# The epsilon of four variances moved from ScalarE to GpSimd, with a new order of all steps, in a four-layer attention kernel

## The chip, the cores and the metric

One core of one Trainium2 chip runs the whole program. The metric is the time of one execution on the device, in microseconds (us); lower is better. Engines are called by the names of the profile: PE is TensorE (matmuls and transposes through a matmul with the identity), PEld its loading of weights, DVE is VectorE, ACT is ScalarE, POOL is GpSimd, SP is SyncE, whose instruction queue SPq issues every DMA of this kernel. The PE clock that the throttle granted was full (2.4 GHz) in the whole stage that matters, so nothing below is about the clock.

## What is computed

Four layers of cross-attention over 64 batch elements of 128 tokens with 256 features. The keys and values of all four come from `ctx_512` (128 features); the second layer also attends to a side input. Cut to what matters (`softmax` over keys in L0, L1 and L3, over tokens in L2):

```python
def attn(q, k, v): return softmax(q @ k.T * scale) @ v
def ln(x, g, b, eps): return (x - mean(x)) * rsqrt(var(x) + eps) * g + b

# L0
x = x + attn(x@Wq+bq, ctx@Wk+bk, ctx@Wv+bv) @ Wo + bo
# L1: two attentions, on ctx and on the side input; eps = 1e-5
x1n = ln(x, ln1_g, ln1_b)
out = x + sum(attn(x1n@Wq+bq, ln(s)@Wk+bk, ln(s)@Wv+bv) @ Wo + bo for s in (ctx, side))
x = ln(out, ln_g, ln_b) @ fc_W + fc_b + out
# L2: eps = 1e-6
x = ln(x + attn_over_tokens(x, ctx), gamma, beta)
# L3
x = x + attn(x@Wq+bq, ctx@Wk+bk, ctx@Wv+bv) @ Wo + bo
```

So there are four kinds of variance, which the kernel calls `keys` (of ctx and side), `ln1` (of the queries of L1), `lnf` (in front of fc) and `ln2` (the end of L2). Each needs `(var + eps) ** -0.5`.

## The kernel before

The 64 batch elements are worked on in 32 groups of two (`GROUPS`, `GROUP`; numbers g from 0 to 31). For each group about 100 named steps run, each on one engine: for example `Q_L0` (queries of L0) on PE, `exp_L1` on ACT, `out_L0` on DVE, `lo_L0` on POOL. The steps of up to a dozen groups are under way together. Ahead of and among the first groups stand the preparations (`PREPARATIONS`): weights are loaded, multiplied with each other (`M_L0`, `N_L1a`, ...), centred and split into a high and a low part.

The order is written out by hand in tables: `STARTS` has a number for each step and group, `PREPARATIONS` one for each preparation. `timetable()` sorts all of them, and each engine gets its own steps in that sequence. The numbers do nothing but sort; no instruction waits for a time. `SEATS` says which of the 8 PSUM banks a PE step fills. `COPIES` says how many buffers a tile has, and a step waits (`earlier`) until the buffer that it takes is free. Between engines every step waits for the semaphores of those it reads (`done[...]`).

The reciprocal roots are made as follows. For `keys`, `lnf` and `ln2`, DVE takes `bn_stats` and `bn_aggr` (`moments`, L1407; the second raises `mean_k`), ACT adds epsilon (`eps_of`, L1118, one `ACTIVATE` with the tile `epsilon` as its bias, which writes `var_eps`), POOL raises it to the power -0.5 (`rstd_of`, L1646, the instruction at L1655). For `ln1` the sum comes from `out_L0`; DVE turns it into `less_mean_ln1` (L1447), ACT squares and sums (`eps_ln1`, L1135), then scales by 1/256 and adds epsilon in a further `ACTIVATE` (L1140), and POOL takes the power. What follows is `shift_keys` (L1464) and `shift_ln2` (L1472) on DVE, `norm_side` (L1664) and `norm_ln2` (L1674) on POOL, `norm_ctx` (L1230) and `norm_ln1` (L1238) on ACT, and `out_fc` (L1507) on DVE. An epsilon step has 128x2 or 128x4 values.

All DMAs are issued by SP in the order of the table: the loads of weights and of the first groups, then, among the loads, each group's trips through HBM that turn a tile (`send_keys` and `fetch_keys`, `send_x3` and `fetch_x3`, `send_xhat` and `fetch_xhat`), and `store`. At the start the table has SP load ctx of group 0, the weights of L2's queries and keys (`load_qk_L2`), two rows, and the columns of small vectors (`load_cols`, one DMA with 34 values a partition). PE begins with `run_up` (L802), then `M_L2` (L784), `k_L2` (L794, which needs DVE's `scaled` of the columns), `B2` of group 0 (L865, which needs both parts of `M_L2`, made by ACT and DVE), `M_L0` (L706).

Of the kernel before, what the change touches and what calls it, by code (L numbers as in the profile page):

```python
# [1793 lines left out]
```

## Time and profile before

| | us |
|---|---|
| median of 3 runs | 564.6 (562.73 to 564.97) |
| the profiled execution | 563.27 |
| its span, from first to last instruction | 561.4 |

| engine | busy us | share | instructions |
|---|---|---|---|
| PE | 545.0 | 97% | 4308 |
| PEld | 524.9 | 93% | 4308 |
| DVE | 479.8 | 85% | 1533 |
| ACT | 479.7 | 85% | 1698 |
| POOL | 416.0 | 74% | 545 |

A matmul with float32 operands is recorded as two, so the counts of PE are above those of the program. A PE record overlaps the next one, since the array is pipelined: the ends are modelled, and a busy PE is one that always had something under way. The 16 DMA engines carry 92.3 MB at 164 GB/s on average.

### The profile page before, as it was taken

The page shows a single profiled execution, that of the slowest core. Times are in us where ns is not written, and L with a number is a line of the kernel's source. Part 1 is how long each engine was busy: PE and PEld are TensorE (multiplying, and loading weights), DVE is VectorE, ACT ScalarE, POOL GpSimd, SP SyncE. Part 2 cuts the span into 40 slices and gives each one's busy share as a digit, 9 for nine tenths or more (in the row PEclk, how much of TensorE's full clock was granted, in tenths as well). Part 3 has the DMA queues.
Part 4 walks back from the last instruction along what each step waited for, and adds up shares of the span by engine and source line. Part 5 has one row for each costly group of instructions (what it writes and reads, how often), then busy time and mean ns, then how long its engine had stood idle before and what let it go on. Part 6 is the DMA issues. An engine that isn't in the chain of part 4 may idle for free.

```text
span 561.4 us, 16080 instructions
## 1 busy us (share of the span) xinstructions
PE 545.0 (97%) x4308; PEld 524.9 (93%) x4308; DVE 479.8 (85%) x1533; ACT 479.7 (85%) x1698; POOL 416.0 (74%) x545
## 2 busy tenths in 40 slices
PE   7998999999999999999999999999999999999985
PEld 6998999999999999999999999999999999999974
DVE  1697689998999989988898998999997979889963
ACT  3798998899988999989989799979879998897643
POOL 3799567888858969587896878866998657365781
PEclk9999999999999999999999999999999999999999
DMA  8994254555475455654547553655476334333332
GB/s 237 361 298 157 85 162 139 174 172 158 148 219 187 145 171 169 207 165 160 165 151 238 158 165 113 215 191 167 146 211 187 110 123 133 109 99 115 95 95 75
DMA packets 100648, 92.30 MB, mean 164 GB/s; under 512 B 10576, under 2 KB 76496, under 8 KB 100560
## 3 DMA queue, kind: packets, MB, share of 16 engines
q1 hardware_dynamic: 100560, 91.29, 51.5%
q8 instruction: 36, 0.59, 0.4%
q14 instruction: 52, 0.43, 0.3%
HBM read 58.74 MB, written 32.51 MB: 163 GB/s over the span
## 4 chain that ended last, share of the span: by engine, by line
PE 83%; POOL 3%; issue 3%; DMA 3%; DVE 3%; ACT 3%; SPq 1%; DVEq 0%; POOLq 0%; ACTq 0%
PE bank L828 10%; PE bank L841 9%; PE bank L835 9%; PE bank L852 5%; PE bank L854 5%; PE bank L853 5%; PE bank L962 5%; PE bank L1005 5%; PE bank L819 5%; PE bank L811 4%; PE bank L984 4%; PE bank L865 3%; PE bank L937 3%; PE bank L938 3%; PE bank L939 3%
## 5 line engine op out<-in xcount | busy, mean ns | idle before, releaser
L1114 ACT ACTIVATE prob_L<-bank,neg_max_L 128x128 f32<-128x128 f32 x320 | 114.6, 376 | 13.3 <-DVE neg_max_L L1480 12.9
L1655 POOL TENSOR_TENSOR rstd_ln<-var_eps_ln,minus_half 128x2 f32<-128x2 f32 x64 | 45.2, 706 | 35.8 <-ACT var_eps_ln L1124 17.8
L1114 ACT ACTIVATION_READ_ACCUMULATOR prob_L<-bank,neg_max_L 128x1 f32 x320 | 69.0, 216 | 0.0
L1480 DVE TENSOR_REDUCE neg_max_L<-bank 128x2 f32<-128x256 f32 (+1 forms) x128 | 60.4, 476 | 6.4 <-PE bank L835 4.8
L1040 ACT ACTIVATE oT_hi_L<-bank 128x256 fp32r<-128x256 f32 (+1 forms) x96 | 44.0, 461 | 12.8 <-PE bank L841 11.1
L1293 DVE TENSOR_TENSOR oT_lo_L<-bank,oT_hi_L 128x256 fp32r<-128x256 f32 (+1 forms) x96 | 47.8, 499 | 7.3 <-ACT oT_hi_L L1040 6.6
L1040 ACT ACTIVATE probT_L<-bank 128x256 f32<-128x256 f32 (+1 forms) x96 | 43.3, 460 | 12.2 <-PE bank L819 11.9
L1703 POOL TENSOR_TENSOR x_bias<-x,bias_fc 128x512 f32<-128x512 f32 x32 | 41.0, 1281 | 15.3 <-DVE x L1513 15.1
L1696 POOL TENSOR_TENSOR x_in<-x_in,bias_L 128x512 f32<-128x512 f32 x32 | 41.1, 1287 | 11.0 <-DMA x_in<-in_x 11.0
L1513 DVE TENSOR_TENSOR x<-bank,x 128x512 f32<-128x512 f32 x64 | 43.3, 679 | 6.5 <-issue 3.3
L1688 POOL TENSOR_TENSOR xT_lo_L<-xT_in,xT_hi_L 128x512 fp32r<-128x512 f32 x32 | 41.2, 1288 | 7.2 <-ACT xT_hi_L L1040 7.1
L819 PE MATMUL bank<-ident,prob_L 128*128 128x128 f32 x256 | 43.0, 274 | 0.3 <-ACT prob_L L1114 0.2
L1718 POOL TENSOR_TENSOR x_res<-xhat_ln,gamma_row 128x512 f32<-128x512 f32 x32 | 41.1, 1286 | 2.7 <-DVE y L1507 2.1
L1720 POOL TENSOR_TENSOR x_res<-x_res,bias_L 128x512 f32<-128x512 f32 x32 | 41.1, 1284 | 2.5
L852 PE MATMUL bank<-N_hi_L,oT_hi_L 128*128 128x256 f32 x128 | 40.7, 318 | 2.1 <-DVE oT_lo_L L1293 2.1
L1245 ACT ACTIVATE prob_L<-prob_L,inv_total_L 128x128 f32<-128x128 f32 x128 | 41.1, 409 | 0.7 <-DVE inv_total_L L1487 0.5
L1655 POOL TENSOR_TENSOR rstd_keys<-var_eps_keys,minus_half 128x4 f32<-128x4 f32 x32 | 32.6, 1018 | 10.6 <-ACT var_eps_keys L1124 5.2
L835 PE MATMUL bank<-ctx_in,qT_L 128*128 128x128 f32 x256 | 39.3, 276 | 0.3
L841 PE MATMUL bank<-probT_L,ctx_in 128*128 128x128 f32 x256 | 39.0, 277 | 0.6 <-ACT probT_L L1040 0.5
L1674 POOL TENSOR_SCALAR xhat_ln<-x,rstd_ln,shift_ln 128x256 f32<-128x256 f32 x64 | 35.1, 555 | 5.1 <-DVE shift_ln L1472 3.0
L937 PE MATMUL bank<-F_hi,xT_hi_fc 128*128 128x256 f32 x128 | 38.0, 297 | 0.1
L1507 DVE SCALAR_TENSOR_TENSOR y<-bank,inv_total_L,x_res 128x256 f32<-128x256 f32 x64 | 27.8, 476 | 9.6 <-PE bank L854 8.0
(238 smaller groups left out, 2251.0 us busy)
## 6 DMA issues: line engine op xcount, KB each, us to landing
ctx_in<-in_ctx SPq DMA_DIRECT2D x32, 256.0 KB, 3.3
xT_in<-in_x SPq DMA_DIRECT2D x32, 256.0 KB, 3.3
x_in<-in_x SPq DMA_DIRECT2D x32, 256.0 KB, 3.1
keys_out<-keys_turned SPq DMA_DIRECT2D x32, 256.0 KB, 2.3
keysT<-keys_out SPq DMA_DIRECT2D x128, 64.0 KB, 2.1
out<-y SPq DMA_DIRECT2D x32, 256.0 KB, 2.2
x_out<-x_turned SPq DMA_DIRECT2D x30, 256.0 KB, 2.2
x3T<-x_out SPq DMA_DIRECT2D x120, 64.0 KB, 2.1
```

Source lines behind the costliest of these rows:

```text
L819: last = tr(block(bank, b), src[:, b, :], ident[:])
L828: last = mm(bank[:, i * TOK:(i + 1) * TOK], w[:, t, :], x[:, t, :], start=t == 0 and n == 0, stop=t == T - 1 and n == 2)
L835: last = mm(block(bank, b), block(at(qT[k], g), b), kT[:, b], start=True, stop=True)
L841: last = mm(block(bank, b), natural[:, b, :], block(at(probT[k], g), b), start=True, stop=True)
L852: mm(to, h, N_h[:], start=i == 0, stop=False)
L937: mm(to, hi[:, t, s], F_hi[:, t, :], start=t == 0, stop=False)
L1040: activation(to, of, ACT.Copy).then_inc(done[step], 1)
L1114: last = activation(at(prob[k], g)[:, b, :], block(bank, b), ACT.Exp, bias=at(neg_max[k], g)[:, b:b + 1], accum_out=at(total[k], g)[:, b:b ...
L1293: dve.tensor_tensor(to, of, hi.bitcast(F32), ALU.subtract).then_inc(done[step], 1)
L1480: dve.tensor_reduce(at(neg_max[k], g)[:], scores, AX.X, ALU.max, negate=True).then_inc(done[f"max_{k}"], 1)
L1513: dve.tensor_tensor(flat(at(to, g)), bank_of(use, g)[:], flat(at(add, g)), ALU.add).then_inc(done[step], 1)
L1655: pool.tensor_tensor(at(rstd[k], g)[:], at(var_eps[k], g)[:], minus_half[:, 0:n], ALU.pow).then_inc(done[f"rstd_{k}"], 1)
```

## The change

The epsilon steps leave ACT. `eps_of` and the last instruction of `eps_ln1` are gone, with the two tiles `epsilon` and their memsets; what is left of `eps_ln1` is a step of its own name, `squares_ln1`. In `rstd_of`, POOL now waits for `mean_k` (or `squares_ln1`), adds epsilon with a `tensor_scalar` from one SBUF tile (two operations, multiply and add, for `ln1`), waits for its own write, and takes the power. DVE's `bn_aggr` waits for the buffer's last reader, now `rstd_k` instead of `eps_k`.

All tables (`STARTS`, `PREPARATIONS`, `SEATS`) have new numbers; `COPIES` has not. The new sequence differs most in the first transfers and the preparations. Behind that, the places of most steps change by a few, and the last steps on PE stand in the old sequence.

```diff
-            def eps_of(k, eps):
-                def of(g):
-                    if g == 0:
-                        prepared(act, "constants")
-                    act.wait_ge(done[f"mean_{k}"], g + 1)
-                    earlier(act, f"rstd_{k}", g, len(var_eps[k]))
-                    activation(at(var_eps[k], g)[:], at(mean_var[k], g)[:, :, 1], ACT.Identity,
-                               bias=epsilon[eps][:, 0:1]).then_inc(done[f"eps_{k}"], 1)
-                return of
...
-                act.wait_ge(done["squares_ln1"], g + 1)
-                earlier(act, "rstd_ln1", g, len(var_eps["ln1"]))
-                activation(at(var_eps["ln1"], g)[:], at(squares_ln1, g)[:], ACT.Identity, bias=epsilon[EPS_L1][:, 0:1],
-                           scale=1.0 / D).then_inc(done["eps_ln1"], 1)
...
-                earlier(dve, f"eps_{k}", g, len(mean_var[k]))
+                earlier(dve, f"rstd_{k}", g, len(mean_var[k]))
...
-            def rstd_of(k, used_by):
-                def of(g):
+            def rstd_of(k, used_by, epsilon, of):
+
+                def rstd_k(g):
                     if g == 0:
                         prepared(pool, "constants")
+                    pool.wait_ge(done[of], g + 1)
+                    if k == "ln1":
+                        pool.tensor_scalar(at(var_eps[k], g)[:], at(squares_ln1, g)[:], 1.0 / D, epsilon, ALU.mult, ALU.add).then_inc(done[f"eps_{k}"], 1)
+                    else:
+                        pool.tensor_scalar(at(var_eps[k], g)[:], at(mean_var[k], g)[:, :, 1], epsilon, None, ALU.add).then_inc(done[f"eps_{k}"], 1)
                     pool.wait_ge(done[f"eps_{k}"], g + 1)
...
-    "load_qk_L2": 118, "load_cols": 310, "load_rows_wkv_L1v": 214, "load_qk_L1v": 406, "load_qk_L0": 502, "load_v_L2": 598,
...
+    "load_qk_L2": 70, "load_rows_wkv_L1v": 598, "load_cols": 214, "load_qk_L1v": 502, "load_qk_L0": 310, "load_v_L2": 406,
```

How the order moves. First, SP at the start of the program, before and then after (line numbers of the changed kernel are lower by 7 to 21; `WqT_L2` is the weight of L2's queries, `WqT_L0` that of L0's):

```order
L640 DMA ctx_in_0<-in_ctx 128x512
L577 DMA WqT_L2<-in_L2_WqT 128x2x256
L577 DMA WkT_L2<-in_L2_WkT 128x2x128
L581 DMA row_L1v_g2<-in_rows 128x128
L581 DMA row_L1v_b2<-in_rows 128x128
L600 DMA cols<-in_cols 128x34
L644 DMA side_in_0<-in_side 128x256
```

```order
L570 DMA WqT_L2<-in_L2_WqT 128x2x256
L570 DMA WkT_L2<-in_L2_WkT 128x2x128
L633 DMA ctx_in_0<-in_ctx 128x512
L593 DMA cols<-in_cols 128x34
L627 DMA xT_in_0<-in_x 128x512
L570 DMA WqT_L0<-in_L0_WqT 128x2x256
L570 DMA WkT_L0<-in_L0_WkT 128x2x128
```

The weights of L2 now go first instead of second and third, and the columns fourth instead of sixth; the two rows and the side input are later.

Second, PE at the start of the program, behind `run_up`: before and then after (`WqT_L,WkT_L` is `M_L2`, `ctxT_hi,M2T_hi` and the like are `B2` of group 0, `scaled_cols,WqT_L` is `k_L2`):

```order
L784 MATMUL bank<-WqT_L,WkT_L 128x256 x2
L794 MATMUL bank<-scaled_cols,WqT_L 128x1 x4
L865 MATMUL bank<-ctxT_hi,M2T_hi 128x256
L865 MATMUL bank<-ctxT_hi,M2T_lo 128x256
L865 MATMUL bank<-ctxT_lo,M2T_hi 128x256
```

```order
L777 MATMUL bank<-WqT_L,WkT_L 128x256 x2
L858 MATMUL bank<-ctxT_hi,M2T_hi 128x256
L858 MATMUL bank<-ctxT_hi,M2T_lo 128x256
L858 MATMUL bank<-ctxT_lo,M2T_hi 128x256
L858 MATMUL bank<-ctxT_hi,M2T_hi 128x256
L858 MATMUL bank<-ctxT_hi,M2T_lo 128x256
L858 MATMUL bank<-ctxT_lo,M2T_hi 128x256
L787 MATMUL bank<-scaled_cols,WqT_L 128x1 x4
L699 MATMUL bank<-WkT_L,WqT_L 128x128 x4
```

`B2` of group 0 now stands ahead of `k_L2`; `M_L0` (`WkT_L,WqT_L`) follows both as before.

Third, POOL some 40 instructions in, where the first groups of L0 and L1 overlap the preparations: before and then after (`rstd_ln1_1` is the buffer 1 of `rstd_ln1`):

```order
L1688 TENSOR_TENSOR xT_lo_L0_0<-xT_in_1,xT_hi_L0_0 128x512
L1664 TENSOR_SCALAR keys_2<-side_in_2,rstd_keys_0 128x128 x2
L1682 TENSOR_TENSOR ctxT_lo_0<-ctx_in_4,ctxT_hi_0 128x256
L1655 TENSOR_TENSOR rstd_ln1_1<-var_eps_ln1_1,minus_half 128x2
L1655 TENSOR_TENSOR rstd_keys_1<-var_eps_keys_1,minus_half 128x4
L1655 TENSOR_TENSOR rstd_ln1_0<-var_eps_ln1_0,minus_half 128x2
```

```order
L1661 TENSOR_TENSOR ctxT_lo_0<-ctx_in_4,ctxT_hi_0 128x256
L1643 TENSOR_SCALAR keys_2<-side_in_2,rstd_keys_0 128x128 x2
L1628 TENSOR_SCALAR var_eps_ln1_1<-squares_ln1_1 128x2
L1634 TENSOR_TENSOR rstd_ln1_1<-var_eps_ln1_1,minus_half 128x2
L1619 TENSOR_TENSOR row_L3_bo<-row_L3_bo,row_L3_b1 128x256
L1630 TENSOR_SCALAR var_eps_keys_1<-mean_var_keys_1 128x4
L1634 TENSOR_TENSOR rstd_keys_1<-var_eps_keys_1,minus_half 128x4
L1628 TENSOR_SCALAR var_eps_ln1_0<-squares_ln1_0 128x2
L1634 TENSOR_TENSOR rstd_ln1_0<-var_eps_ln1_0,minus_half 128x2
```

Each power now has its epsilon in front of it on the same engine, 128 of them in the program, and a row of the preparations (`row_L3_bo`) has moved in among them.

## Rows read from the trace of the kernel before

**Rows 1.** The page, busy time of each engine, share of the span, instructions.
```profile
PE 545.0 (97%) x4308; PEld 524.9 (93%) x4308; DVE 479.8 (85%) x1533; ACT 479.7 (85%) x1698; POOL 416.0 (74%) x545
```

**Rows 2.** Stretches: length, busy us (instructions) of PE, PEld, DVE, ACT, POOL; clock, DMA, GB/s.
```profile
0.00:20.00 20.00, 16.67 (x77) 15.13 (x78) 5.96 (x23) 7.99 (x19) 9.52 (x27) 1.00 0.89 272
20.00:50.00 30.00, 29.42 (x219) 27.73 (x220) 24.41 (x93) 28.13 (x94) 27.65 (x36) 1.00 0.89 285
50.00:80.00 30.00, 27.95 (x231) 26.84 (x230) 22.91 (x77) 27.86 (x97) 19.17 (x23) 1.00 0.37 117
...
100.00:520.00 420.00, 418.39 (x3404) 407.66 (x3403) 380.54 (x1200) 379.30 (x1361) 319.63 (x412) 1.00 0.52 162
520.00:561.00 41.00, 33.16 (x231) 29.19 (x230) 27.07 (x82) 19.34 (x68) 24.60 (x32) 0.98 0.28 89
```

**Rows 3.** Groups of ACT: the epsilon steps; busy us, mean ns, idle before <-releaser.
```profile
L1124 ACT ACTIVATE var_eps_keys<-mean_var_keys,epsilon 128x4 f32<-128x4 f32 x32 | 9.9, 311 | 2.1 <-DVE mean_var_keys L1416 2.1
L1124 ACT ACTIVATE var_eps_lnf<-mean_var_lnf,epsilon 128x2 f32<-128x2 f32 x32 | 9.8, 307 | 1.9 <-DVE mean_var_lnf L1416 1.8
L1124 ACT ACTIVATE var_eps_ln<-mean_var_ln,epsilon 128x2 f32<-128x2 f32 x32 | 9.7, 303 | 0.9 <-DVE mean_var_ln L1416 0.7
L1140 ACT ACTIVATE var_eps_ln<-squares_ln,epsilon 128x2 f32<-128x2 f32 x32 | 9.5, 296 | 1.0
```

**Rows 4.** The same view of POOL.
```profile
L1655 POOL TENSOR_TENSOR rstd_ln<-var_eps_ln,minus_half 128x2 f32<-128x2 f32 x64 | 45.2, 706 | 35.8 <-ACT var_eps_ln L1124 17.8 <-ACT var_eps_ln L1140 17.7
...
L1720 POOL TENSOR_TENSOR x_res<-x_res,bias_L 128x512 f32<-128x512 f32 x32 | 41.1, 1284 | 2.5
...
L1674 POOL TENSOR_SCALAR xhat_ln<-x,rstd_ln,shift_ln 128x256 f32<-128x256 f32 x64 | 35.1, 555 | 5.1 <-DVE shift_ln L1472 3.0 <-issue 2.1
...
L1664 POOL TENSOR_SCALAR keys<-side_in,rstd_keys 128x128 f32<-128x128 f32 x64 | 23.2, 375 | 9.1 <-PE bank L841 8.8 <-POOL rstd_keys L1655 0.4
...
L1588 POOL MEMSET one<- 128x1 f32 x1 | 0.1, 99 | 0.0
```

**Rows 5.** The power (L1655) on POOL by stretch: length, busy (instructions), clock, DMA, GB/s.
```profile
20.00:50.00 30.00, 6.08 (x7) 1.00 0.89 285
...
100.00:520.00 420.00, 79.73 (x103) 1.00 0.52 162
```

**Rows 6.** Timeline at the start: start us, us, what [idle before <-releaser]; SP, ACT, PE.
```profile
1.66 0.46 SPq L577 DMA_DIRECT2D WkT_L<-in_L_WkT  x1
...
7.81 0.39 ACT L1104 ACTIVATE M2T_hi<-bank 128x256 fp32r<-128x256 f32 x1 [3.95 <-PE bank L784]
...
5.70 2.08 PE L784 MATMUL bank<-WqT_L,WkT_L 128*128 128x256 f32 x4 [1.79 <-DMA WkT_L<-in_L_WkT]
8.34 1.87 PE L794 MATMUL bank<-scaled_cols,WqT_L 128*128 128x1 f32 x8 [0.56 <-DVE scaled_cols L1297]
```

**Rows 7.** The chain that ended last: start us, us, what.
```profile
3.14 4.93 DMA cols<-in_cols
...
38.32 0.30 ACT var_eps_ln L1140
...
39.43 1.03 POOL M_lo_L1a L1627
...
48.55 1.03 POOL rstd_keys L1655
```

**Rows 8.** Timelines of DVE, POOL and PE from 49 to 53 us.
```profile
49.62 2.46 DVE L1464 SCALAR_TENSOR_TENSOR shift_keys<-mean_var_keys,rstd_keys,one 128x1 f32<-128x1 f32 x2
...
49.53 1.30 POOL L1688 TENSOR_TENSOR xT_lo_L<-xT_in,xT_hi_L 128x512 fp32r<-128x512 f32 x1
50.77 1.28 POOL L1696 TENSOR_TENSOR x_in<-x_in,bias_L 128x512 f32<-128x512 f32 x1
...
52.73 0.39 PE L828 MATMUL bank<-xT_hi_L,M_hi_L1a 128*128 128x256 f32 x1 [1.46 <-DVE xT_lo_L L1293]
```

**Rows 9.** Line L1464 of DVE: duration ns min/median/max.
```profile
L1464 DVE SCALAR_TENSOR_TENSOR shift_keys<-mean_var_keys,rstd_keys,one x64: 176/213/1306, 11.3 to 475.8; 128x1 f32<-128x1 f32 x64
```

More of the change, by code:

```diff
@@ new lines @@
+    "rstd_keys": [1426, 2077, 2870, 4535, 5226, 5809, 6545, 7370, 8941, 11613, 13273, 14563, 15378, 16048, 18933, 20861, 21391,
[59 rows of a table added]
+    "T_fc": [5972, 6945, 7838, 9006, 10690, 13100, 14169, 15159, 16461, 18051, 20719, 21677, 23079, 24381, 26606, 27727, 29880,
[3 rows of a table added]
+    "hi_fc": [6185, 7069, 7905, 9069, 10798, 13178, 14234, 15292, 16553, 18178, 20790, 21823, 23187, 24444, 26718, 27819, 29973,
+        30998, 33455, 35009, 35786, 36720, 38447, 40383, 42823, 44998, 45831, 46724, 48787, 49725, 50647, 51348],
@@ new lines @@
+    "OUT_fc": [6433, 7219, 8042, 9341, 11099, 13748, 14531, 15618, 16778, 18423, 21086, 22206, 23555, 24831, 27302, 28242,
+        30238, 31568, 33917, 35260, 35966, 37221, 38884, 40633, 43090, 45232, 46107, 46886, 49034, 49877, 51056, 51751],
+    "out_fc": [6600, 7381, 8284, 9523, 11262, 13923, 14719, 15780, 17053, 18629, 21496, 22369, 23717, 25078, 27482, 28481,
[33 rows of a table added]
+    "x_res": [8678, 10145, 11350, 12602, 13873, 16857, 18598, 19245, 20472, 21527, 24086, 25678, 27197, 27997, 30482, 32080,
[17 rows of a table added]
+    "store": [10772, 12223, 14749, 15490, 19065, 20202, 20763, 22614, 23234, 26797, 27151, 29011, 29428, 32031, 34357, 35378,
[7 rows of a table added]
@@ L234 @@
-PREPARATIONS = {"run_up": 154, "M_L2": 461, "k_L2": 669, "M_L0": 950, "m_L0": 1039, "M_L1v": 1104, "n_fc": 1193, "mean_fc": 1280,
[14 rows of a table removed]
[1 row of a table added]
+    "turn_xhat": [8617, 10047, 11115, 12500, 13830, 16761, 17934, 19263, 20036, 21342, 24115, 25608, 27133, 28296, 30402, 32118,
+        33773, 34676, 38056, 38891, 39860, 41329, 41806, 43709, 45632, 47893, 49087, 50432, 51582, 52152, None, None],
+    "send_xhat": [8694, 10181, 11313, 12606, 13908, 16839, 18012, 19392, 20250, 21420, 24414, 25758, 27210, 28435, 30479, 32196,
+        33851, 34754, 38133, 38969, 39970, 41465, 41932, 43787, 46053, 47970, 49165, 50510, 51660, 52230, None, None],
@@ new lines @@
+    "fetch_xhat": [9032, 10447, 11578, 12927, 14173, 17104, 18285, 19658, 20571, 21758, 24824, 26024, 27499, 28771, 30877,
[5 rows of a table added]
+    "shift_keys": [1570, 2245, 3014, 4719, 5381, 6026, 6942, 7930, 9126, 11757, 13518, 14797, 15669, 16247, 19089, 21462, 22082,
+        22905, 25374, 26721, 28559, 29540, 30602, 33189, 34601, 36857, 38175, 38275, 40990, 42704, 44183, 45478],
+    "norm_ctx": [1615, 2290, 3125, 5601, 6448, 7164, 8575, 10358, 12984, 13734, 14528, 15952, 17992, 20285, 20964, 22664, 24010,
+        26044, 27069, 29179, 30214, 32640, 34329, 35313, 35919, 37839, 39566, 42140, 43887, 45094, 45879, 48015],
@@ new lines @@
+    "norm_side": [1574, 2603, 4286, 5614, 6289, 7193, 8429, 10640, 12971, 14136, 14700, 15873, 17584, 20028, 21103, 22621,
+        23898, 26047, 27927, 29130, 30170, 32603, 34286, 35395, 35922, 37955, 39472, 42187, 43957, 45049, 45852, 48218],
+    "load_xT": [262, 1366, 1414, 1462, 2374, 3046, 3620, 4103, 4917, 5628, 7806, 9464, 10639, 12010, 12558, 14845, 15810, 17344,
[3 rows of a table added]
+}
+PREPARATIONS = {"run_up": 154, "M_L2": 421, "k_L2": 868, "M_L0": 1045, "m_L0": 1364, "M_L1v": 1628, "n_fc": 1453, "mean_fc": 1540,
[14 rows of a table added]
@@ L251 @@
 SEATS = {
     "M_L2": [0],
-    "k_L2": [1],
-    "B2": [2, 3, 6, 1, 6, 2, 4, 3, 4, 5, 1, 3, 0, 6, 7, 3, 6, 4, 2, 1, 6, 1, 2, 2, 6, 6, 0, 7, 0, 1, 5, 6],
+    "k_L2": [2],
+    "B2": [1, 6, 7, 3, 3, 4, 0, 0, 0, 7, 2, 1, 7, 7, 0, 3, 3, 5, 7, 6, 4, 3, 1, 0, 7, 6, 2, 4, 3, 2, 0, 6],
     "M_L0": [3],
-    "m_L0": [4],
-    "M_L1v": [5],
+    "m_L0": [5],
+    "M_L1v": [0],
     "n_fc": [6],
     "mean_fc": [7],
[26 rows of a table removed]
-    "T_fc": [5, 0, 2, 6, 1, 3, 5, 0, 6, 7, 5, 6, 4, 0, 1, 7, 2, 7, 1, 0, 3, 3, 2, 0, 6, 6, 3, 1, 4, 0, 2, 1],
@@ L346 @@
 ONLY_LATE = ("hi_L2", "xT_L3")
-SMALL = [f"{what}_{k}" for what in ("stats", "mean") for k in ("keys", "lnf", "ln2")] + ["squares_ln1"] + ["x_gamma", "zeroed", "small"]
+SMALL = [f"{what}_{k}" for what in ("stats", "mean") for k in ("keys", "lnf", "ln2")] + [f"eps_{k}" for k in ("keys", "ln1", "lnf", "ln2")] + ["x_gamma", "zeroed", "small"]
 def timetable():
@@ L386, in build @@
         scaled_cols = sb("scaled_cols", [P, len(COLS), T])
-        epsilon = {e: sb(f"epsilon_{i}", [P, 1]) for i, e in enumerate((EPS_L1, EPS_L2))}
         gamma_row = sb("gamma_row", [P, D])
@@ L1116, in exponentials, with squares_ln1_of @@
                 last.then_inc(done[f"exp_{k}"], 1)
[L1118 to L1131 removed]
+            def squares_ln1_of(g):
                 act.wait_ge(done["less_mean_ln1"], g + 1)
                 earlier(act, "T_L1", g, len(xhat["ln1"]))
+                earlier(act, "rstd_ln1", g, len(squares_ln1))
                 for b in range(GROUP):
@@ L1281, in scalar_program @@
                       "hi_L1": hi_of("L1", "Q_L1"), "hi_fc": hi_of("fc", "OUT_fc"),
-                      "xT_L3": xT_L3, "eps_keys": eps_of("keys", EPS_L1), "eps_ln1": eps_ln1,
-                      "eps_lnf": eps_of("lnf", EPS_L1), "eps_ln2": eps_of("ln2", EPS_L2)},
+                      "xT_L3": xT_L3, "squares_ln1": squares_ln1_of},
                      {f"M_hi_{a}": M_hi_of(a) for a in ATTENTIONS if a != "L3"} | {f"N_hi_{a}": N_hi_of(a) for a in ATTENTIONS}
@@ L1445, in mean_ln1 @@
                 dve.wait_ge(done["out_L0"], g + 1)
-                earlier(dve, "eps_ln1", g, len(less_mean_ln1))
+                earlier(dve, "squares_ln1", g, len(less_mean_ln1))
                 dve.tensor_scalar(at(less_mean_ln1, g)[:], at(sum_ln1, g)[:], -1.0 / D, None, ALU.mult).then_inc(done["less_mean_ln1"], 1)
@@ L1585, in constants @@
                                    channel_multiplier=1)
-                for eps, tile in epsilon.items():
-                    pool.memset(tile[:], eps)
                 pool.memset(one[:], 1.0)
@@ L1720, in x_res_of @@
                 pool.tensor_tensor(at(x_res, g)[:], at(x_res, g)[:], every(bias["L3"]), ALU.add).then_inc(done["x_res"], 1)
-            steps_of({"rstd_keys": rstd_of("keys", "norm_side"), "rstd_ln1": rstd_of("ln1", "norm_ln1"),
-                      "rstd_lnf": rstd_of("lnf", "out_fc"), "rstd_ln2": rstd_of("ln2", "norm_ln2"),
+            steps_of({"rstd_keys": rstd_of("keys", ["norm_side", "norm_ctx"], EPS_L1, "mean_keys"), "rstd_ln1": rstd_of("ln1", ["norm_ln1"], EPS_L1, "squares_ln1"),
+                      "rstd_lnf": rstd_of("lnf", ["out_fc"], EPS_L1, "mean_lnf"), "rstd_ln2": rstd_of("ln2", ["norm_ln2"], EPS_L2, "mean_ln2"),
                       "norm_side": norm_side, "norm_ln2": norm_ln2, "lo_ctx": lo_ctx, "lo_L0": lo_L0,
```

82 lines of the change are left out of this document (27 added, 55 removed), and 401 rows, old and new, of tables (PREPARATIONS, SEATS, STARTS).

## The prediction

> **What bounds the kernel now.** I read the page first. PE is busy for 545.0 of 561.4 us and no other engine above 85% [rows 1]. A share is an average, so next come the stretches [rows 2]. From 100 to 520 us PE is busy for 418.39 of 420 us: there it sets the pace, and all that the other engines do differently can bring 1.6 us there at most. The rest of PE's idle time lies at the two ends. In the first 20 us it is 20 - 16.67 = 3.3 us, from 20 to 50 us 0.6, from 50 to 80 us 2.05, and behind 520 us 7.8 us. So the ends are what a new order can win or lose.
>
> In these ends other engines are near their limit. From 20 to 50 us ACT is busy for 28.13 us and POOL for 27.65 us of 30; from 50 to 80 us ACT still for 27.86, POOL for only 19.17 [rows 2]. The chain that ended last says which of them counts: from 39.43 us, where POOL splits a weight, to the end of `rstd_keys` at 49.58 us it runs through POOL's own instructions and short gaps in it [rows 7]. Then DVE takes over, with something odd. Two `shift_keys` instructions of one element each took 2.46 us together [rows 8]; the median of one is 213 ns, the shortest 176, the longest 1306 [rows 9]. They ran exactly as long as POOL's two big instructions beside them, 1.30 and 1.28 us. PE then stood for 1.46 us, waiting for DVE [rows 8]. So a DVE instruction whose inputs all lie in SBUF can be held up by a POOL instruction.
>
> **The epsilon on ACT.** What goes is 9.9 + 9.8 + 9.7 + 9.5 = 38.9 us of ACT [rows 3], 479.7 to about 441 us. From 100 to 520 us it lies beside PE's work and is worth nothing but part of the 1.6 us: I take 0. From 50 to 80 us, where six powers stand and ACT has 2.1 us to spare, six steps of 0.30 us make ACT 1.8 us shorter. PE's idle time there is 2.05 us, 1.46 of it the wait of [rows 8], which is DVE's. What is left is 0.6 us and what POOL gives back below; I take -0.6.
>
> "VectorE: DVE Perf Modes" of the Trainium skill (on the TRN2 errata) gives an ScalarE instruction from SBUF to SBUF 224 cycles plus one an element, at 1.2 GHz; for two elements that is an estimate of 188 ns, and 128 of them would give ACT back 24 us. The trace has about 304 ns for the same thing, so the sum goes by 38.9.
>
> **The epsilon on POOL.** The trace shows no `tensor_scalar` of two elements on POOL. Two of its rows have that operation, 375 ns at 128 elements and 555 ns at 256 [rows 4]; the line through them is 195 ns plus 1.4 ns an element, so 0.20 us. Its bounds are the memset of one element, 0.10 us, and the 128-element instruction, 0.375 us. Then POOL waits for its own write. The nearest case is `x_res`, whose second half waits for its first: 2.5 us idle in 32, so 0.08 us [rows 4]. Together 0.28 us a step (0.1 to 0.46), 128 steps: 36 us (13 to 59). POOL goes from 416.0 busy to about 441 us, 79%.
>
> In the middle stage there are 103 powers [rows 5], so 29 us more beside 319.63 of 420 us [rows 2]: 349, or 83%. POOL also waits less: 35.5 us it stood in front of the powers of `ln1` and `ln2` was a wait for ACT's epsilon alone [rows 4], and now it waits for DVE or the squares directly, one hand-over earlier. The steps behind the roots are hidden by the groups under way. I take 0 here, with bounds of -1.6 (all of PE's idle time) and +3 (two holds as in rows 8).
>
> From 20 to 50 us it is otherwise. Seven powers stand there [rows 5], 7 x 0.28 = 2.0 us, and POOL has 2.35 us to spare. Since the chain runs through POOL here, I count it on the path: five of the seven are behind 38 us, +1.4 us. Against it stands the one epsilon step of ACT that is on the chain, 0.30 us, and the hand-over to POOL, about 0.1 [rows 7]: -0.4. Sum +1.0, with bounds of 0 (the new order of the preparations gives POOL air) and +2.
>
> The two holds of `shift_keys` cost PE 1.46 us. Whether they come back depends on what POOL runs at that instant. Normal would be 0.4 us for the pair instead of 2.46. POOL will be no less busy, but the coincidence was a rare one (longest of 64). I take half of it as gone, -0.7; bounds -1.5 and +1.5.
>
> **The first transfers.** `WkT_L` of L2 is now second in SP's queue instead of third. The queue takes 0.5 us an entry (third at 1.66 us [rows 6]), so `M_L2` can start at 5.2 instead of 5.70 us. The columns landed at 3.14 + 4.93 = 8.07 us [rows 7]; two places earlier make it about 7.1, and the 0.56 us that `k_L2` waited [rows 6] are gone. But `B2` now stands first, and it needs both parts of `M_L2`. ACT's part took 0.39 us [rows 6], DVE's has the same size, and with hand-overs the wait is about 1.0 us from the end of `M_L2`. So PE wins 0.5 us, trades a wait of 0.56 for one of 1.0, and then has the same products to make: -0.1 us. Bounds: -1.1 (both waits gone), and +1.5 if SP stops at the second weights of L3. That load stands 12 issues earlier and waits until PE has made `M_L0` and `m_L0`; ctx of group 4 and the weights `L1a` queue behind it. SP gets there at 0.7 + 30 x 0.5 = 15.7 us, about when `m_L0` ends behind `V_L2`, so I take no wait.
>
> **The end.** The last 22 steps of PE stand in the old order. Each last root comes a little earlier, 0.30 us on ACT against 0.28 on POOL and one hand-over less: -0.1.
>
> **The sum.** -0.6 + 0 + 1.0 - 0.7 - 0.1 - 0.1 = -0.5 us. Against the profiled execution, 563.27 us (span 561.4 and 1.9 around it), this is 562.8. The median of the runs lies 1.3 us above it, so I put it at 564.1 for a median: no change that can be told.
>
> **The rivals.**
> 1. *The start gets in step with its transfers.* If the new order fits what really lands when, PE's idle time of 3.3 + 0.6 + 2.05 us is roughly halved (-3.0), and the preparations spread POOL's load. With -0.6 from the middle: 564.6 - 3.6 = 561.0. For it: PE waits at the start for exactly two transfers [rows 6], and both come earlier. Against it: POOL and ACT were at 92 and 94% from 20 to 50 us, not the DMAs alone.
> 2. *POOL becomes the bound of the start, and holds DVE up.* Place: 20 to 55 us. Price: all seven steps on the path, +2.0, and one more hold of `shift_keys` or `less_mean` of 1.3 to 1.5 us there, since POOL would be busy for 29.6 of 30 us: +3.4, so 568.0. It decides once the epsilon steps take more than the 2.35 us that POOL has to spare, which is at 0.34 us a step, within my bounds. For it: the chain goes through POOL. Against: from 50 to 80 us POOL has 10.8 us to spare [rows 2], into which late work can slide. "GPSIMD Engine Reference" of the Trainium skill (the table in section 1) says that GpSimd and VectorE share their SBUF interface, with contention for DVE instructions of two SBUF inputs or in a mode that uses both ports; by that rule, with which rows 8 agree, `shift_keys` is exposed and `max` or `bn_stats` are not.
> 3. *SP stops at L3's weights.* +1.5: 566.1, still within what counts as the same.
>
> **How the numbers follow.** The forecast (564.1, with about 2 us to either side) and rival 3 have 0.60 together, rival 1 0.22, rival 2 0.18. A measurement of this kernel can tell about 0.5%, or 2.8 us, from no change: faster is below 561.8, slower above 567.4. The range has to take in all but 2 in 10: from 560.8 (rival 1) to 567.6, which cuts rival 2's upper part. Faster 0.22, same 0.60, slower 0.18.
>
> **What would show it.** ACT's busy time at 441 us with no `var_eps` in its groups, POOL's at 441 us with a new group of 128 at about 0.2 us: right on the prices. PE's busy time unchanged and its stretch from 100 to 520 us again short of full by 1 to 3 us: right on the middle. `M_L2` at 5.2 us and `B2` about 1 us behind its end: right on the transfers. From 20 to 50 us POOL above 29 us busy, PE waiting for DVE or POOL by more than 2 us in all: rival 2. PE's idle time in the first 80 us near 3 us: rival 1. SP waiting for PE at about 15 us: rival 3. The prediction is wrong above all if the start of the groups, between 20 and 80 us, moves by more than 3 us, or if the middle stage shows waits of PE that it does not have now.

## The result, and the profile after

The changed kernel took **569.9 us** (median; 569.0 to 573.0) beside 563.9 us for the kernel before on the same chip: a ratio of 1.012, 95% interval 1.007 to 1.016. It is slower by about 6 us, where 564.1 was forecast and 567.6 was the upper end of the range. The profiled execution took 570.6 us, its span is 568.8. Ratios leave out executions in a slower state of the chip; there was one, in the run below whose median is given as 562.0 us (561.7 without it).

The page's engine totals, to be read beside [rows 1]:

```profile
PE 546.2 (96%) x4308; PEld 524.4 (92%) x4308; DVE 488.9 (86%) x1533; ACT 458.2 (81%) x1570; POOL 448.3 (79%) x671
```

The stretches (length, busy us and records of PE, PEld, DVE, ACT, POOL; clock, DMA share, GB/s), beside [rows 2]:

```profile
0.00:20.00 20.00, 17.31 (x90) 15.99 (x91) 7.98 (x35) 9.51 (x23) 11.80 (x29) 0.83 0.86 273
20.00:50.00 30.00, 29.13 (x224) 27.43 (x223) 24.25 (x81) 27.41 (x91) 27.89 (x40) 1.00 0.89 293
50.00:80.00 30.00, 27.36 (x224) 26.47 (x225) 25.01 (x82) 26.67 (x85) 21.76 (x33) 1.00 0.36 119
...
100.00:520.00 420.00, 412.92 (x3336) 400.35 (x3336) 378.06 (x1176) 356.95 (x1242) 341.34 (x507) 1.00 0.51 160
```

PE idles for 7.1 of the 420 us in the middle, where it idled for 1.6, and starts 3336 matmuls there instead of 3404. At some 0.12 us each, 68 fewer are 8 us. Against the kernel before nothing is lost by the end of the start: 90 matmuls in the first 20 us against 77. Counted one by one, the 300th matmul begins 3.1 us earlier than before, the 1000th 0.2 us earlier, the 3000th 5.6 us later and the 3500th 7.7 us later. The granted clock in the first 20 us was 0.83 (1.00 before), a mean of the two levels of 2.4 and 1.2 GHz; it can't be the loss, since PE is ahead of before at 20 us.

ACT lost 21.5 us and not 38.9, POOL got 32.3, and DVE, whose instructions are the same, is busy for 9.1 us more. The groups of its three small steps (busy us, mean ns | idle before) say where. First after, then before:

```profile
L1441 DVE SCALAR_TENSOR_TENSOR shift_keys<-mean_var_keys,rstd_keys,one 128x1 f32<-128x1 f32 x64 | 27.2, 464 | 1.1 <-POOL rstd_keys L1634 1.0
L1424 DVE TENSOR_SCALAR less_mean_ln<-sum_ln 128x2 f32<-128x2 f32 x32 | 10.6, 332 | 0.2
L1449 DVE SCALAR_TENSOR_TENSOR shift_ln<-mean_var_ln,rstd_ln 128x2 f32<-128x2 f32 x32 | 9.7, 304 | 0.1
```

```profile
L1464 DVE SCALAR_TENSOR_TENSOR shift_keys<-mean_var_keys,rstd_keys,one 128x1 f32<-128x1 f32 x64 | 17.8, 317 | 3.4 <-POOL rstd_keys L1655 3.4
L1447 DVE TENSOR_SCALAR less_mean_ln<-sum_ln 128x2 f32<-128x2 f32 x32 | 11.3, 353 | 0.1
L1472 DVE SCALAR_TENSOR_TENSOR shift_ln<-mean_var_ln,rstd_ln 128x2 f32<-128x2 f32 x32 | 7.8, 245 | 1.1 <-POOL rstd_ln L1655 1.0
```

`shift_keys` costs 9.4 us more, `shift_ln2` 1.9 more and `less_mean_ln1` 0.7 less. The line of `shift_keys` in the changed kernel (min/median/max ns), beside [rows 9]:

```profile
L1441 DVE SCALAR_TENSOR_TENSOR shift_keys<-mean_var_keys,rstd_keys,one x64: 177/216/1377, 13.9 to 476.4; 128x1 f32<-128x1 f32 x64
```

The shortest and the median are those of before; the mean isn't. Taken one by one from the trace, 20 of the 64 last at least 0.25 us longer than the shortest, against 7 before, and their durations above the shortest sum to 18.4 us, against 9.0. This is the hold of [rows 8], and one in the middle stage looks like this (timelines: start us, us; DVE, POOL, PE):

```profile
306.93 2.02 DVE L1441 SCALAR_TENSOR_TENSOR shift_keys<-mean_var_keys,rstd_keys,one 128x1 f32<-128x1 f32 x2
308.88 0.68 DVE L1490 TENSOR_TENSOR x<-bank,x 128x512 f32<-128x512 f32 x1
...
306.43 1.28 POOL L1667 TENSOR_TENSOR xT_lo_L<-xT_in,xT_hi_L 128x512 fp32r<-128x512 f32 x1
307.66 1.27 POOL L1682 TENSOR_TENSOR x_bias<-x,bias_fc 128x512 f32<-128x512 f32 x1
...
309.70 0.35 PE L967 MATMUL bank<-Wv_hi,ctxT_hi 128*128 128x256 f32 x1 [0.64 <-DVE x L1490]
```

The first of the two `shift_keys` ends when `xT_lo_L` does, the second with `x_bias`; `x` comes 1.6 us late, and PE stands for 0.64 us. The chain that ended last runs through the second (start, us, what):

```profile
307.65 1.30 DVE shift_keys L1441
```

What PE waited for between 60 and 540 us (us in all, times, longest), the largest of after and then of before:

```profile
PE bank L998 <- DMA xhatT<-xhat_out: 1.6, 3, 0.9
PE bank L845 <- DVE oT_lo_L L1270: 1.4, 3, 0.7
PE bank L804 <- DVE x L1490: 1.1, 1, 1.1
```

```profile
PE bank L962 <- issue: 0.3, 1, 0.3
PE bank L852 <- DVE oT_lo_L L1293: 0.3, 1, 0.3
```

All of PE's waits for DVE in this stretch sum to 5.9 us, against 0.5 before. So the trace says that DVE is late in the middle and that the holds are more and sum to more. It does not say whether the holds are the cause, nor whether POOL's new work or the new order made them.

### The profile page after: what moved, and what is told of

The parts are those of the page before. It is cut to its first block, busy times and chain, and to the rows that moved or that the text cites. A ratio compares the mean times of both kernels' runs of the same rounds, so it can differ in the third digit from the quotient of the medians.

```text
span 568.8 us, 15954 instructions
## 1 busy us (share of the span) xinstructions
PE 546.2 (96%) x4308; PEld 524.4 (92%) x4308; DVE 488.9 (86%) x1533; ACT 458.2 (81%) x1570; POOL 448.3 (79%) x671
## 4 chain that ended last, share of the span: by engine, by line
PE 65%; DVE 7%; DMA 6%; issue 5%; POOL 3%; SPq 2%; ACT 1%; DVEq 0%; POOLq 0%; ACTq 0%
PE bank L821 8%; PE bank L834 7%; PE bank L828 7%; PE bank L845 5%; PE bank L955 4%; PE bank L847 4%; PE bank L846 4%; PE bank L804 4%; PE bank L998 4%; PE bank L977 4%; PE bank L812 3%; DMA xhat_out<-xhat_turned 3%; PE bank L930 2%; DMA xhatT<-xhat_out 2%; PE bank L931 2%
## 5 line engine op out<-in xcount | busy, mean ns | idle before, releaser
L834 PEld LDWEIGHTS bank<-probT_L,ctx_in 128*128 128x128 f32 x256 | 34.0, 191 | 2.4 <-ACT probT_L L1033 2.1
```

The source lines that it names most:

```text
L834: last = mm(block(bank, b), natural[:, b, :], block(at(probT[k], g), b), start=True, stop=True)
```

## The experiments

All times are medians; the kernel before had 563.7 to 565.3 us in these sessions. A ratio is to it, with its 95% interval. A difference between two of the kernels is mostly one between sessions, so one of 1 or 2 us can't be told from nothing.

### Order and placement apart

The new code with the tables of before (the squares at the place of the old `eps_ln1`), and the old code with the new tables:

```
# old order, epsilon on POOL: STARTS, PREPARATIONS, SEATS of before
-    "eps_ln1": [3158, 3860, ...
+    "squares_ln1": [3158, 3860, ...
# new order, epsilon on ACT
+for k, later in (("keys", 228), ("lnf", 158), ("ln2", 125)):
+    STARTS[f"eps_{k}"] = [min(stats + later, rstd - 1) for ...]
```

> The code of after (epsilon on POOL) with the order of before: all three tables are those of before, the squares stand where the squares and the epsilon of ln1 stood, and the three other epsilon steps have no place of their own. Three theories. Theory H (holds): POOL is busy for 32 us more, so DVE instructions with SBUF inputs alone are held up more often behind POOL's long ones (after: shift_keys 18.4 us above its shortest time against 9.0 before, 20 of 64 held against 7), DVE falls behind and PE waits. Then this kernel loses most of the 6 us: 567 to 570 us, shift_keys at least 15 us above its shortest. Theory P (the steps themselves on POOL's queue, later roots): the same time, 567 to 570, but with the holds as before. Theory O (the new order alone): this kernel is as fast as before, 563 to 565 us, with PE at 418 of 420 us in the middle stage.

> The code of before (epsilon on ACT) with the order of after; the epsilon steps of keys, lnf and ln2 stand as far behind their statistics as the median of before had them, and those of ln1 directly behind the squares. Theory O (the new order alone costs it): 568 to 571 us, PE idle for 5 to 8 us from 100 to 520 us, and shift_keys held about as often as in after. Theories H and P (POOL's load): 563 to 566 us, PE again near 418 of 420.

Measured: 576.8 us (1.024, 1.018 to 1.029) and 572.7 us (1.015, 1.010 to 1.020). Both are above what any theory had for them. The first is slower than both pure kernels; the second is slower than the kernel before, and its interval overlaps that of the changed one (1.007 to 1.016). So neither "the order" nor "the epsilon" is the answer alone. `shift_keys` in the first and the second:

```profile
L1441 DVE SCALAR_TENSOR_TENSOR shift_keys<-mean_var_keys,rstd_keys,one 128x1 f32<-128x1 f32 x64 | 21.0, 369 | 6.3 <-POOL rstd_keys L1634 6.1
...
L1462 DVE SCALAR_TENSOR_TENSOR shift_keys<-mean_var_keys,rstd_keys,one 128x1 f32<-128x1 f32 x64 | 26.9, 460 | 1.0 <-POOL rstd_keys L1653 1.0
```

With the new order it has 26.9 us although POOL is as lightly loaded as before; with the old order 21.0 although POOL has the epsilon. Above the shortest that is 18.2 and 11.6 us. **The order makes the holds, not POOL's load.** Counted by what POOL was running when a `shift_keys` began: a `TENSOR_TENSOR` other than the power (0.7 to 1.3 us long) with at least 0.15 us left was under way at 7 of the 64 before, 16 after, 15 in the new order with epsilon on ACT, and 11 in the old order with it on POOL. All of these 49 lasted until POOL's instruction ended, within some 30 ns. A power with as much left was under way at 34 of them in the four kernels, and none of these lasted longer than 0.22 us. So the power does not hold DVE. A `TENSOR_SCALAR` was under way at 31, of which 13 were held.

### The holds taken out

`shift_keys` with another instruction at the same place, with the same waits and outputs:

```
                 for n in range(GROUP):
-                    last = dve.scalar_tensor_tensor(out=at(shift["keys"], g)[:, n:n + 1], in0=at(mean_var["keys"], g)[:, n, 0:1],
-                                                    scalar=at(rstd["keys"], g)[:, n:n + 1], in1=one[:, 0:1], ...)
+                    last = dve.reciprocal(at(shift["keys"], g)[:, n:n + 1], at(rstd["keys"], g)[:, n:n + 1])
```

(The weights don't take the other shift out again, as the expectation has it. These kernels have other values in the ctx keys of L1, over the same instructions elsewhere.)

> After, with another instruction in shift_keys: two reciprocals of rstd_keys in place of the two instructions with SBUF inputs for mean, root and one. Same waits, same output tile, same number of instructions, about 155 ns instead of a median of 207. The tile then holds a different constant shift of each key, which the centred weights of L1 take out again. Reciprocals show no hold in the trace of after. Theory H: DVE is busy for about 20 us less, PE's waits for DVE in the middle stage go from about 7 us to 3 or 4, and the time is 565 to 567.5 us. Theories P and O: DVE's holds are not what PE waits for, the time stays at 569 to 571.

> Before, with the same other instruction in shift_keys. DVE is busy for 10 us less. PE is the bound in the middle stage of before, so all theories expect little: 562.5 to 564.5 us. Most of it is the 1.46 us that PE waited at 51 to 53 us, which go if the two held shift_keys there were their cause; if the time does not move at all, something else was ready as late.

Measured: 562.0 us (0.995, 0.992 to 0.999) and 562.9 us (0.997, 0.994 to 1.000). The first gained more than any theory allowed. The line of the new order now reads

```profile
L1441 DVE RECIPROCAL shift_keys<-rstd_keys x64: 121/146/165, 14.1 to 467.3; 128x1 f32<-128x1 f32 x64
```

with none longer than 165 ns, though 32 of the 64 begin beside a `TENSOR_TENSOR` of POOL with 0.15 us or more left. Without the holds of this one step the changed kernel gains 7.9 us, the kernel before 1.5, and the two are the same. PE's matmuls started in the first 100 us (columns: length, PE busy, clock, DMA, GB/s), after and then this kernel:

```profile
0.00:100.00 100.00, 92.53 (x685) 0.97 0.63 205
```

```profile
0.00:100.00 100.00, 96.12 (x724) 0.98 0.67 214
```

39 matmuls more by 100 us, 4 to 5 us: so over half of what the holds cost was lost in the start already, and the middle lost the rest. PE's waits for DVE between 60 and 540 us are 0.9 us instead of 5.9. But this kernel's middle is not that of before:

```profile
100.00:520.00 420.00, 413.88 (x3370) 403.48 (x3369) 372.97 (x1185) 356.71 (x1245) 341.88 (x510) 1.00 0.51 160
```

PE is still idle for 6.1 us there, and starts 3370 matmuls against 3404. Its 400th matmul begins 5.7 us earlier than before, its 2500th 5.2 us, its 3500th only 0.7 us. So the new order wins 5 to 6 us at the start and loses most of it again late in the middle, without `shift_keys` being held. The kernel with no epsilon step below does the same (6.0, 4.4 and 0.4 us ahead). What costs this wasn't tried; `less_mean_ln1` and `shift_ln2` are still held in both.

The same exchange in the two mixtures:

> New order with the epsilon on ACT (572.7 us), and the reciprocals in shift_keys (changed shift of the ctx keys). shift_keys lost 18.2 us there by holds, as in after. Theory H: 564 to 567 us. If the order itself is at fault in another way (theory O), 569 to 572 us.

> Old order with the epsilon on POOL (it took 576.8 us), and the reciprocals in shift_keys (which changes the shift of the ctx keys, as above). If holds are what the old order loses by the epsilon on POOL too (theory H), it comes down to 563 to 566 us. If it is POOL's queue, in which the steps now stand at the place of the old power and the roots come later than the rest was planned for (theory P), it loses only some 3 us: 572 to 575 us.

567.0 us (1.002, 0.999 to 1.005) in place of 572.7, and 573.2 (1.014, 1.009 to 1.018) in place of 576.8. The holds cost 5.7 and 3.6 us there. The new order pays 6 to 8 us for them, the old 1.5 to 4, wherever the epsilon stands. The old order with the epsilon on POOL stays at 573: something else costs it 10 us.

### POOL's added time

The same kernels with no epsilon step at all:

```
-                    pool.tensor_scalar(at(var_eps[k], g)[:], at(mean_var[k], g)[:, :, 1], epsilon, None, ALU.add)...
-                    pool.wait_ge(done[f"eps_{k}"], g + 1)
-                    pool.tensor_tensor(at(rstd[k], g)[:], at(var_eps[k], g)[:], minus_half...
+                    pool.tensor_tensor(at(rstd[k], g)[:], at(squares_ln1, g)[:] if k == "ln1" else at(mean_var[k], g)[:, :, 1], minus_half...
```

> The old order with the reciprocals in shift_keys (573.2 us with the epsilon on POOL, 562.9 with it on ACT), and now with no epsilon step at all: POOL takes the power straight from the variance (the epsilon, and for ln1 the division by 256, are left out, and the shift of the ctx keys is changed as before). POOL is busy for about 415 us again and ACT for 440. Theory P1: the 10 us are the time of POOL's 128 added instructions in an order planned without them; then 561 to 564 us. Theory P2: they come from what else the epsilon on POOL changes (the root waits for DVE directly, the buffer of the mean is held longer, ACT's sequence without its epsilon steps); then it stays above 568.

> The same edit in the new order (562.0 us with reciprocals and the epsilon on POOL): no epsilon step at all. If POOL's 32 us are on nobody's path in the new order, 560.5 to 562.5 us; if POOL's time counts in the new order too, as theory P1 has it for the old one, 556 to 559.

558.6 us (0.990, 0.985 to 0.995) and 558.9 (0.991, 0.988 to 0.994). The medians form a table, all with the reciprocals in `shift_keys`, and with the real step in brackets:

| | old order | new order |
|---|---|---|
| no epsilon step | 558.6 | 558.9 |
| epsilon on ACT | 562.9 (564.4) | 567.0 (572.7) |
| epsilon on POOL | 573.2 (576.8) | 562.0 (569.9) |

Free of the holds of `shift_keys` and of the epsilon, the two orders take the same time. The same 128 instructions of POOL, 32 us, cost 14.6 us in the old order and 3.1 in the new; the 128 of ACT cost 4.3 in the old and 8.1 in the new. Each order suits the placement that it came with, and the change as a whole is free: 562.0 against 562.9. P1 holds for the old order, where it expected 561 to 564 and the gain was even larger. The 558.9 us of the new order lie where POOL's time counts there too (556 to 559), but the intervals with and without the epsilon overlap, so the 3.1 us are only just told from nothing. That the new order has its steps where POOL has time for them is what the table suggests; which steps they are was not tried.

### Sum of DVE's time, or length and moment

The reciprocals took 16 us off DVE (488.9 to 472.9). To give that back without holds, more reciprocals were put in:

```
+                for n in (4, 5, 2, 3, 0, 1):       # three small ones for one, unused columns
+                    last = dve.reciprocal(at(shift["keys"], g)[:, n:n + 1], ...)
```

> The kernel with reciprocals in shift_keys (new order, epsilon on POOL), with four more reciprocals a group into unused columns of the same tile, so that DVE has its work back but not its holds: 128 x about 0.15 us = 19 us more, DVE busy for about 492 us, as in after (488.9). As in that kernel, the shift of the ctx keys is another value than the reference's. Theory H1 (DVE was simply too busy; the holds count by their sum): 568 to 571 us. Theory H2 (a hold costs by its length and the moment, 1.2 us at once in front of what PE waits for): 562 to 565 us.

562.6 us (0.995, 0.993 to 0.997). It told little: the small ones ran on top of each other, and DVE was busy for 478.1 us, only 5.2 more. Next, one long one in front of each:

```
+                    dve.reciprocal(at(filler, g)[:, n, :], mean_of_D[:])      # 128x128
```

> After with reciprocals in shift_keys (562.0 us; changed shift of the ctx keys) and, in front of each of them, one more reciprocal of 128x128 values into a tile that nobody reads. The five added small reciprocals tried before ran nearly on top of each other and gave DVE only 5 of the 16 us back. One of 128x128 values should take 0.2 to 0.25 us, so 64 of them 13 to 16 us: DVE busy for 486 to 489 us, as in after (488.9), but in pieces of 0.25 us and none of 1.3. Theory H1 (the sum of DVE's time): 568 to 571 us. Theory H2 (long holds at a bad moment): 562 to 565.

588.6 us (1.041, 1.038 to 1.044), against both theories, as the filler was four times as long as meant:

```profile
L1442 DVE RECIPROCAL filler<-mean_of_D 128x128 f32<-128x128 f32 x64 | 57.9, 935 | 0.2 <-POOL rstd_keys L1634 0.2
```

That is 26.6 us for 58 us of filler, 0.46 us a us, the same rate as the holds (7.9 us for 16.7 us, which is the 18.4 above the shortest less the 1.7 that the reciprocals show): a point for the sum. So about the same total was tried in two shapes, 64 short pieces, and 16 long ones, two in a row in every fourth group:

```
+                    dve.reciprocal(at(filler, g)[:, n, 0:28], mean_of_D[:, 0:28])
...
+                    if g % 4 == 3:
+                        dve.reciprocal(at(filler, g // 4)[:, n, :], mean_of_D[:])
```

> After with reciprocals in shift_keys (562.0 us; changed shift of the ctx keys) and, in front of each of the 64, a reciprocal of 128x28 values that nobody reads. The one of 128x128 took 935 ns, 64 of them 58 us of DVE, and cost 26.6 us: 0.46 us a us. This one is sized for about 0.25 us on DVE, 16 us in all, as much as the holds of shift_keys took in after, but evenly spread and in short pieces. Theory H1 (the sum of DVE's time counts, 0.46 of it): 562.0 + 7.4 = 569.4, at least 567.5. Theory H2 (a long piece at a bad moment counts, short ones are absorbed): 562 to 564.5.

> The same 15 us of filler on DVE, but in 16 pieces of 0.93 us: the reciprocal of 128x128 only in every fourth group, in front of both of its shift_keys, a pattern close to the holds of after (20 of 0.3 to 1.3 us, often two in a row). H1: as the even filler, 568 to 570. H2: 568 to 570 here too, and 4 us or more above the even filler.

561.3 us (0.995, 0.993 to 0.998) and 569.1 (1.009, 1.006 to 1.013). Their fillers, and the first 100 us of PE, even and then in lumps:

```profile
L1442 DVE RECIPROCAL filler<-mean_of_D 128x28 f32<-128x28 f32 x64 | 18.0, 312 | 1.3 <-POOL rstd_keys L1634 1.1
...
0.00:100.00 100.00, 95.87 (x723) 0.98 0.67 214
```

```profile
L1443 DVE RECIPROCAL filler<-mean_of_D 128x128 f32<-128x128 f32 x16 | 14.5, 936 | 0.0
...
0.00:100.00 100.00, 93.39 (x689) 0.97 0.64 206
```

DVE was busy for 480.6 and 482.6 us. The even one costs nothing that can be told from 562.0, the lumps 7.1 us. PE's waits for DVE between 60 and 540 us sum to 1.3 and 5.0 us. In the first 100 us the lumped kernel starts 689 matmuls, about as many as after (685), the even one 723, as the kernel without holds (724). **Sixteen stalls of DVE by 0.93 us, in eight pairs and with no POOL in it, cost about what the holds cost.** This is theory H2. Neither filler brings DVE back to the 488.9 us of the changed kernel, but between the two, 2.0 us of DVE's time stand beside 7.8 us of the program's. Where a piece falls was chosen only by group, so how much the moment counts beside the length stays open.

### Versions that compute the whole reference

The first took all three exposed steps off DVE: squares of `sum - 256 x` on ACT (no `less_mean_ln1`), `norm_ln2` by the mean and the root (no `shift_ln2`), `shift_keys` on POOL.

```
-                    ... at(rstd["ln2"], g)[:, n:n + 1], at(shift["ln2"], g)[:, n:n + 1], ALU.mult, ALU.add)
+                    ... at(mean_var["ln2"], g)[:, n, 0:1], at(rstd["ln2"], g)[:, n:n + 1], ALU.subtract, ALU.mult)
...
+                pool.tensor_tensor(to, at(mean_var["keys"], g)[:, 0:GROUP, 0], at(rstd["keys"], g)[:, 0:GROUP], ALU.mult)...
+                pool.tensor_scalar(to, to, -1.0, 1.0, ALU.mult, ALU.add)...
```

> After without any of DVE's three small exposed steps, computing the whole reference: the squares are taken of sum - 256 x, so that less_mean_ln1 is not needed; norm_ln2 subtracts the mean and multiplies by the root, so that shift_ln2 is not needed; shift_keys goes to POOL as two instructions of about 0.24 us. DVE loses 10.6 + 29.7 + 9.7 = 50 us, of which 30.7 us were holds, and POOL gets 32 x 0.5 = 16 us more, to about 464 us (82%). Theory H: at least as good as the version with reciprocals, 556 to 563 us. If POOL's load is a bound of its own (theory P), it stays above 566 us.

592.1 us (1.046, 1.042 to 1.050). `norm_ln2` in its new form:

```profile
L1637 POOL TENSOR_SCALAR xhat_ln<-x,mean_var_ln,rstd_ln 128x256 f32<-128x256 f32 x64 | 78.0, 1226 | 0.7 <-POOL rstd_ln L1607 0.7
```

1226 ns instead of 555 [rows 4], 43 us more of POOL (502.1 busy). Whether the subtraction or the mean's place in memory does that wasn't tried. Without that edit, in both orders:

> After with two of the three exposed steps gone from DVE, computing the whole reference: the squares are taken of sum - 256 x (no less_mean_ln1), and shift_keys is made on POOL by two instructions of 0.20 us (multiply, then multiply and add). shift_ln2 and norm_ln2 stay as they are (in the version without shift_ln2, norm_ln2 took 1226 instead of 555 ns an instruction, 43 us more of POOL, and 592 us). DVE is busy for about 448 us, POOL for 462. Theory H2 (the long holds are what costs): 559 to 564 us. Theory P: POOL's time counts, and shift_keys comes later by POOL's queue: 566 to 571.

> The same two edits in the kernel before (epsilon on ACT, old order). POOL is busy for 430 us, DVE for 448. Few holds stood on the path there: H2 gives 561 to 564 us, theory P (POOL's added instructions cost more than they take, as the epsilon did in this order) 566 to 570.

565.0 us (1.001, 0.998 to 1.004) and 562.2 us (0.997, 0.994 to 1.000): the changed kernel gains 4.9 us and is level with before, 1 us above what H2 had for it; the kernel before gains a little, just above what can be told. Of its two edits alone,

> The kernel before, only without less_mean_ln1 (the squares are taken of sum - 256 x; the whole reference is computed). It is one of the two edits of the version that took 562.2 us, and takes 11.3 us of DVE away, 7.2 of them holds, and adds nothing to POOL. If that edit brought the gain: 561.5 to 563 us. If it was shift_keys on POOL: 563.5 to 564.5.

gave 565.2 us, beside 565.3 for before (0.999, 0.997 to 1.001): nothing, though it takes 7.2 us of holds away. If the small gain is real, it would be that of `shift_keys` on POOL; the intervals of the two overlap, so this isn't shown. Nothing that computes the whole reference came below 562.

## Why the prediction was wrong

**The step that failed** is the term on DVE's holds: "the coincidence was a rare one (longest of 64). I take half of it as gone, -0.7; bounds -1.5 and +1.5". With it fails the middle stage, "I take 0 here, with bounds of -1.6 (all of PE's idle time) and +3 (two holds as in rows 8)". The mechanism was named, also as one hold more in rival 2, but it was counted as one event between 49 and 53 us. It was 7 events of 64 before already, and 20 after. The view of groups would have shown it: 17.8 us for 64 instructions whose shortest is 0.176 us [rows 9], 6.5 us more than 64 times the shortest, for busy time in which overlaps count once. The holds of `shift_keys` measured 7.9 us after and 1.5 before, so +6.4 in place of -0.7. In the middle PE's idle time grew by 5.5 us in place of 0, past the bound of +3, and its waits for DVE from 0.5 to 5.9 us.

**The rest of the sum** is +0.2 without the term on holds; measured without these holds it is -0.9 (562.0 against 562.9). That they are near each other is in part luck. The forecast had about nothing for the first transfers and nothing for the middle; without the holds of `shift_keys` PE is 5.7 us ahead at its 400th matmul and 0.7 us at its 3500th. Two effects of some 5 us, neither of them in the sum, take each other out.

**Rival 2** had the right engines and the wrong cause and place. It made the holds depend on POOL's fuller time from 20 to 55 us. POOL was busy for 27.89 us from 20 to 50 (27.65 before), and the holds follow the order with a light POOL too. Of the 20 held, 9 lie in the first 100 us, 4 of them behind 55 us; before, it was 4 and none. "GPSIMD Engine Reference" of the Trainium skill (table in section 1) has GpSimd and VectorE share their SBUF interface, with contention for DVE instructions of two SBUF inputs or in a two-port mode. The runs agree for DVE's side: `shift_keys` is held (20 of 64), reciprocals at its place never are (0 of 64). They add that on POOL's side the power, 0.7 to 1.0 us long, held none of the 34 that began beside it.

**ACT.** 38.9 us were to go; 21.5 went, 0.168 us a step. The duration of a record, 0.30 us, isn't what the engine gets back. The durations of all records of ACT, taken one by one and added up, fell by 38.3 us; but in the kernel before the next record starts ahead of the epsilon's end in 94 of 128 cases, and busy time counts overlaps once. "VectorE: DVE Perf Modes" of the Trainium skill (on the TRN2 errata) led to an estimate of 24 us; the prediction set it aside for the row, and the 21.5 us measured stand nearer to that estimate.

**POOL.** The step was priced at 0.20 + 0.08 us and measured

```profile
L1628 POOL TENSOR_SCALAR var_eps_ln<-squares_ln 128x2 f32<-128x2 f32 x32 | 6.2, 195 | 6.7 <-ACT xhat_ln L1117 4.4
L1630 POOL TENSOR_SCALAR var_eps_lnf<-mean_var_lnf 128x2 f32<-128x2 f32 x32 | 7.4, 231 | 2.0
L1634 POOL TENSOR_TENSOR rstd_ln<-var_eps_ln,minus_half 128x2 f32<-128x2 f32 x64 | 45.5, 711 | 5.3
```

at 195 to 240 ns, with 5.3 us idle before 64 powers, 0.08 each: right. The sum, "about 441", is 416 + 128 x 0.20, without the waits; the four new groups measured 28.7 us (those of 128x4 take 240 ns), the powers 1.3 us more, and POOL 448.3 in all. The "+1.0" for these steps from 20 to 50 us isn't seen: without any epsilon step PE reaches its 400th matmul only 0.3 us sooner than with them on POOL, both without the holds of `shift_keys`. That this time is worth nothing in the middle was right for the new order (3.1 us in the whole program) and would have been wrong for the old (14.6): "the steps behind the roots are hidden by the groups under way" has no row behind it.

**The transfers.** PE, DVE and SP at the start, beside [rows 6]:

```profile
4.21 1.13 PE L777 MATMUL bank<-WqT_L,WkT_L 128*128 128x256 f32 x4 [0.30 <-DMA WkT_L<-in_L_WkT]
6.75 0.37 PE L858 MATMUL bank<-ctxT_hi,M2T_hi 128*128 128x256 f32 x1 [1.41 <-DVE scaled_cols L1274]
...
6.18 0.42 DVE L1278 SCALAR_TENSOR_TENSOR M2T_lo<-bank,M2T_hi 128x256 fp32r<-128x256 f32 x1 [6.18 <-ACT M2T_hi L1097]
...
1.21 0.46 SPq L570 DMA_DIRECT2D WkT_L<-in_L_WkT  x1
```

`M_L2` began at 4.21 us (5.2 forecast, 5.70 before), since both its transfers went out first; `B2` waited for 1.41 us (1.0 forecast) and began at 6.75. The start gained 2 to 3 us where -0.1 stood: the 90th matmul begins 2.3 us earlier than before, the 400th (at 62 us) 3.1 us. This is rival 1, right for the first 60 us, and by the 600th matmul (at 90 us) all but 0.9 us of it is gone; without the holds it is 6.0 us there. SP didn't stop at L3's weights; its one wait of that kind between 10 and 60 us was 0.2 us, so rival 3 did not happen.

## What to carry to other kernels

Compare the mean of a small instruction with its shortest, not only its longest: the difference times the count is a stall that no wait shows. In this kernel a new order alone doubled that sum (9.0 to 18.2 us) for an instruction that POOL's work can hold, and stalls of 0.93 us in pairs cost 7.1 us where about the same total in 0.3 us pieces was free. A hand-made order belongs to the durations that it was made with: judge a moved instruction and its order together; here either alone lost. And a sum that comes out right can be two large effects that cancel: compare when the same count of matmuls is reached, not only the end.
